# Layer 1 of a four-layer graph kernel attends first and projects the aggregate; VectorE takes four late copies

## The chip, the cores and the metric

The kernel runs on one core of one Trainium2 chip. The metric is the device time of one execution in microseconds. The core has five engines that run their own instruction queues in order and meet at semaphores: TensorE (PE, matrix products into eight PSUM banks), VectorE (DVE), ScalarE (ACT), GpSimd (POOL, which reads and writes SBUF alone here) and SyncE (SP, which issues the transfers of the loop).

## The reference, cut to what matters

`x` is 128 graphs x 128 nodes x 256 features, `adj` one 128x128 matrix for all graphs. Four layers follow, each on `h = relu(layernorm(x))` and each added to `x`:

```python
x = x + L0(h)   # deg * (h Wi^T + b) + adj @ (h Wj^T)
x = x + L1(h)   # single-head attention over nodes, below
x = x + L2(h)   # single-head attention, 128 wide, [alpha @ hh, hh]
x = x + L3(h)   # eight-head attention with q, k, v and output projections

def L1(x, adj, W, a_src, a_dst):
    Wh = einsum('bnd,de->bne', x, W)
    e_src = einsum('bnd,d->bn', Wh, a_src)
    e_dst = einsum('bnd,d->bn', Wh, a_dst)
    logits = leaky_relu(e_src[:, :, None] + e_dst[:, None, :], 0.2)
    logits = where(adj == 0, -inf, logits)
    return einsum('bnm,bmd->bnd', softmax(logits), Wh)
```

## The kernel before

Graphs are handled in pairs (`G = 2`), so there are 64 of them. Nodes lie on the 128 partitions and a pair is 512 columns of f32. In steady state every engine runs `step(t)`, a fixed list of operations, each on the pair `t - LAG[operation]`: one step starts layer 0 of a new pair and ends layer 3 of one eight steps older. `fill()` and `drain()` hold the same operations written out for the first and last pairs. All these lists and the lags, as well as `BANKS`, which says in which PSUM bank a task writes and which operations free it, were laid out ahead of time. `passed` waits for an operation to have reached a pair, `bank_free` for the last user of a bank, `read_before` for the readers of a buffer (most buffers hold two pairs, those of the scores of layer 3 one).

Products that must be exact use a split: a matrix is kept as an upper part rounded to `fp32r` and a lower remainder, and `split_matmul` (L1565 to L1567) adds three products, upper times upper, upper times lower, lower times upper. The products of attention and all transposes are in f32 (each f32 product shows as two instructions, a transpose as one).

Layer 1 of a pair goes as follows. DVE takes statistics of x1, POOL makes `y1 = (x1 - mean) * rstd` (`normalise`, L440). PE transposes y1 (`transpose_y`, L1575, four transposes of 128x128). ACT takes relu and the upper part (L1230), DVE the lower part (`relu_transposed_low`, L821). `project1` multiplies by W, extended by two columns W a_src and W a_dst (258 columns), into one bank per graph; ACT copies both to `wh` (`copy_projection1`, L1258). Column 257 is the destination's logit of every node: POOL gathers it (`gather_dst`, L463), SP writes it to memory and reads it back spread over all partitions (for the first four and last five pairs `spread_dst` does this by a transpose, L1654). ACT adds the source's logit and applies leaky relu (`sum_logits`, L1284), DVE masks it and takes the row's extreme in one `tensor_tensor_reduce` (`mask_logits`, L831), ACT takes exponentials and their sum (L1293), PE transposes them (`transpose_exp`, L1662), ACT copies them (L1301), and `attend` (L1670) multiplies them with `wh`: two f32 products of 256 columns. DVE scales by the inverse sum and adds x1 (`sum_x2`, L847).

Layer 2 has the same stages with 128 columns; its attention product is L1670 with `hh`, its sum `sum_x3` L857, its projection `project2` L1646. Layer 3 projects q, k and v; `add_bias` on DVE (L866) copies q and k from their banks, with the bias; `scores` (L1707) fills four banks, DVE masks them (`mask_scores`, L874), ACT takes exponentials (L1315), POOL normalises (L469), PE transposes four banks (L1715), ACT copies them (`copy_p3_transposed`, L1323), `attend3` (L1727) and `project4` (weights `wo`) follow, and DVE adds (L897).

On PE the step's list is, in order: `project0(1)`, `project4`, the projections to k and q, `project0(0)`, transposes for layers 2 and 3 of older pairs, `attend` of layer 2, `project2`, the transposes of y1, `scores`, `attend3`, the transposes of layer 1's exponentials, `project_v`, `project1(1)`, `attend` of layer 1, `project1(0)`, the transposes of y3, `aggregate`, two more banks of transposed probabilities.

## Time and profile before

| | us |
|---|---|
| time, median of 3 runs | 1220.35 (1220.34 to 1221.02) |
| time of the profiled execution | 1220.8 |
| span from its first to its last instruction | 1218.8 |
| PE busy | 1200.7 (99%) |
| ACT busy | 1082.4 (89%) |
| POOL busy | 1068.4 (88%) |
| DVE busy | 1053.9 (86%) |
| TensorE clock granted, mean share of full speed | 0.999 |

The busy time of an engine counts instructions that do work, not waits. Matmuls overlap in the pipeline of the array, so the time that one costs is read from the start of one to the start of the next, not from its duration.

### The profile page before, as it was taken

What the parts mean: (1) busy time and instruction counts of PE and PEld (TensorE: products, weight loads), DVE (VectorE), ACT (ScalarE), POOL (GpSimd) and SP (SyncE); (2) the same over time, 40 slices, a digit from 0 to 9 for tenths busy, and PEclk for the clock granted to TensorE, in tenths of its full rate; (3) what the DMA queues carried; (4) which work ended last, traced back from release to release, by engine and by line L of the source; (5) the groups of instructions that cost most, each with busy time, mean ns of one, the idle gap of its engine ahead of it and who ended that gap; (6) DMA issues with size and microseconds to landing.
All of it is one profiled execution on the core that took longest, in us unless ns stands there. A gap on an engine that the chain in (4) does not pass through costs nothing.

```text
span 1218.8 us, 43750 instructions
## 1 busy us (share of the span) xinstructions
PE 1200.7 (99%) x12017; PEld 1108.6 (91%) x12017; DVE 1053.9 (86%) x5142; ACT 1082.4 (89%) x3976; POOL 1068.4 (88%) x1848
## 2 busy tenths in 40 slices
PE   8999999999999999999999999999999999999997
PEld 7789999999999999999999999999999999999986
DVE  6898898898898898888988988988988888988874
ACT  3679898898898898898998998998998998998997
POOL 5998899899899898999899899899899899898774
PEclk9999999999999999999999999999999999999999
DMA  7333333343442433534333332432433343330001
GB/s 187 63 46 51 77 68 55 79 67 57 77 67 57 77 67 55 79 64 60 77 63 60 77 65 58 75 68 59 71 69 60 69 67 66 67 51 26 20 20 36
DMA packets 97678, 78.57 MB, mean 64 GB/s; under 512 B 31648, under 2 KB 89248, under 8 KB 97440
## 3 DMA queue, kind: packets, MB, share of 16 engines
q1 hardware_dynamic: 94960, 74.07, 32.9%
q8 instruction: 102, 1.67, 0.8%
q14 instruction: 136, 1.11, 0.6%
q10 hardware_dynamic: 2480, 1.71, 0.5%
HBM read 58.79 MB, written 16.95 MB: 62 GB/s over the span
## 4 chain that ended last, share of the span: by engine, by line
PE 90%; issue 1%; DVE 1%; POOL 0%; ACT 0%; POOLq 0%; DVEq 0%; ACTq 0%
PE bank L1565 16%; PE bank L1567 16%; PE bank L1566 16%; PE bank L1715 9%; PE bank L1670 6%; PE bank L1575 6%; PE bank L1707 6%; PE bank L1727 5%; PE bank L1646 4%; PE bank L1662 3%; PE bank L1626 2%; POOL probs L469 0%; ACT exps L1315 0%; DVE masked L874 0%; PE bank L1654 0%
## 5 line engine op out<-in xcount | busy, mean ns | idle before, releaser
L1315 ACT ACTIVATE exps<-masked,nmax 128x128 f32<-128x128 f32 x1024 | 396.8, 393 | 0.9 <-DVE nmax L874 0.4
L469 POOL TENSOR_TENSOR probs<-exps,rsum 128x512 f32<-128x512 f32 x256 | 266.3, 1042 | 16.2 <-DVE rsum L882 15.7
L440 POOL TENSOR_SCALAR y<-x,nm,rstd 128x256 f32<-128x256 f32 x384 | 212.0, 560 | 31.5 <-issue 31.0
L874 DVE CUSTOM_DVE_ANT_0 masked<-bank,mask 128x128 f32<-128x128 f32 x1024 | 227.4, 284 | 0.8 <-PE bank L1707 0.5
L1315 ACT ACTIVATION_READ_ACCUMULATOR exps<-masked,nmax 128x1 f32 x1024 | 197.3, 193 | 0.0
L760 DVE BATCH_NORM_STATS2 stats<-x 128x6 f32<-128x256 f32 x512 | 190.4, 414 | 4.6 <-DMA x<-in_x 4.4
L1565 PE MATMUL bank<-w_hi,ht_hi 128*128 128x512 f32 (+1 forms) x508 | 189.4, 373 | 0.4 <-DVE ht_lo L821 0.3
L417 POOL TENSOR_TENSOR rstd<-veps,power 128x2 f32<-128x2 f32 x256 | 182.7, 714 | 5.3
L1567 PE MATMUL bank<-w_hi,ht_lo 128*128 128x512 f32 (+1 forms) x508 | 172.6, 340 | 0.0
L1566 PE MATMUL bank<-w_lo,ht_hi 128*128 128x512 f32 (+1 forms) x508 | 172.5, 340 | 0.0
L1323 ACT ACTIVATE probs3t<-bank 128x512 f32<-128x512 f32 x256 | 145.0, 595 | 0.7 <-PE bank L1715 0.7
L1715 PE MATMUL bank<-ident,probs 128*128 128x128 f32 x1024 | 134.3, 273 | 1.2 <-DVE nmax L874 0.8
L1252 ACT ACTIVATE mj_hi<-bank,rstd 128x256 fp32r<-128x256 f32 x128 | 59.8, 468 | 81.5 <-PE bank L1567 78.0
L1715 PEld LDWEIGHTS bank<-ident,probs 128*128 128x128 f32 x1024 | 117.3, 141 | 10.8 <-issue 2.2
L1575 PE MATMUL bank<-ident,y 128*128 128x128 f32 x768 | 115.6, 273 | 4.2 <-POOL y L440 4.1
L1293 ACT ACTIVATE ez<-z,nmax 128x128 f32<-128x128 f32 x256 | 100.2, 394 | 8.0 <-DVE nmax L831 4.4
L1567 PEld LDWEIGHTS bank<-w_hi,ht_lo 128*128 128x128 f32 x508 | 96.1, 189 | 11.7
L781 DVE SCALAR_TENSOR_TENSOR mj_lo<-bank,rstd,mj_hi 128x256 fp32r<-128x256 f32 x128 | 61.2, 479 | 52.6 <-ACT mj_hi L1252 52.5
L1565 PEld LDWEIGHTS bank<-w_hi,ht_hi 128*128 128x128 f32 x508 | 96.6, 190 | 9.3 <-DVE ht_lo L821 1.1
L1566 PEld LDWEIGHTS bank<-w_lo,ht_hi 128*128 128x128 f32 x508 | 96.8, 191 | 7.6
L1575 PEld LDWEIGHTS bank<-ident,y 128*128 128x128 f32 x768 | 89.7, 141 | 6.2 <-POOL y L440 5.7
L857 DVE SCALAR_TENSOR_TENSOR x<-bank,rsum,x 128x128 f32<-128x128 f32 x128 | 39.0, 347 | 60.7 <-PE bank L1670 59.1
(136 smaller groups left out, 3970.4 us busy)
## 6 DMA issues: line engine op xcount, KB each, us to landing
x<-in_x SPq DMA_DIRECT2D x64, 256.0 KB, 5.9
xt_sb<-in_xt SPq DMA_DIRECT2D x64, 256.0 KB, 5.7
out<-x SPq DMA_DIRECT2D x64, 256.0 KB, 5.7
db<-rows SPq DMA_DIRECT2D x110, 128.0 KB, 4.1
mean_b<-rows SPq DMA_DIRECT2D x62, 128.0 KB, 3.4
rows<-dst SPq DMA_DIRECT2D x110, 1.0 KB, 3.6
rows<-mv SPq DMA_DIRECT2D x62, 1.0 KB, 5.8
probs<-in_w0t ACTq DMA_DIRECT2D x1, 256.0 KB, 3.5
```

The lines of the kernel that those rows point to most:

```text
L417: pool.tensor_tensor(rstd[i][:, b], veps[i][:, b], power[:], ALU.pow).then_inc(S[f"rstd{i}"], 1)
L440: last = pool.tensor_scalar(y[i][:, b, g], src[:, bx, g], nm[i][:, s, g:g + 1], rstd[i][:, s, g:g + 1], ALU.add, ALU.mult)
L469: pool.tensor_tensor(probs3[:, p % BUFFERS["probs3"], j], exps3[:, p % BUFFERS["exps3"], j], rsum3[:, s, j].unsqueeze(2).to_broadcast([P, ...
L760: last = dve.bn_stats(stats[i][:, b, g], src[:, bx, g])
L874: last = dve.tensor_tensor_reduce(masked3[:, b, j, i], bank_of(f"sc{j}")[:, i * P:(i + 1) * P], mask[:], scale=-1.0, scalar=-MASKED, op0=A ...
L1315: last = act.activation(exps3[:, b, j, i], masked3[:, p % BUFFERS["masked3"], j, i], ACT.Exp, bias=nmax3[:, s, j, i:i + 1], scale=-1.0, ac ...
L1323: act.activation(probs3t[:, b, j].rearrange("p b n -> p (b n)"), bank_of(f"pt{j}")[:], ACT.Copy).then_inc(S[f"p3t_{j}"], 1)
L1565: pe.matmul(out_ap, lhs[0], rhs[0], start=start, stop=False)
L1566: pe.matmul(out_ap, lhs[0], rhs[1], start=False, stop=False)
L1567: return pe.matmul(out_ap, lhs[1], rhs[0], start=False, stop=stop)
L1575: last = pe.transpose(bank_of(f"h{i}t")[:, (c * G + g) * P:(c * G + g + 1) * P], y[i][:, b, g, c * P:(c + 1) * P], ident[:])
L1715: last = pe.transpose(bank_of(f"pt{j}")[:, i * P:(i + 1) * P], probs3[:, p % BUFFERS["probs3"], j, i], ident[:])
```

## The change

What is computed stays the same. Layer 1 uses that `softmax(..) @ (h W)` is `(softmax(..) @ h) W`, and that `h = relu(x1 - mean) * rstd`, since rstd is positive.

- POOL makes `y1 = max(x1 - mean, 0)` (`centre1`), without rstd.
- The two logits of a node are products of its row with the vectors W a_src and W a_dst. PE spreads these over all partitions of bank 6 once at the start (`a1_rows`), and the bank holds nothing else from then on. DVE makes four `tensor_tensor_reduce` of 256 columns per pair (`logit_products1`), POOL multiplies the four columns of results by rstd (`scale_logits1`). SP writes the destination's logits from there; the gather on POOL is gone.
- The transposes of y1, relu and split of the transposed y1 and the copies to `wh` are gone.
- ACT's copy of layer 1's transposed exponentials multiplies by rstd of the source node, which is its partition there, so one copy becomes two. `aggregate1` multiplies y1 with it, four f32 products of 128 columns whose result is already transposed. ACT and DVE split it (`high_g1`, `low_g1`), and `project1` makes both graphs' 12 products of 256 columns into one bank, from which `sum_x2` reads as before.
- The bias of k is added by ACT (`add_key_bias`) in place of DVE.
- Of the last two pairs, DVE copies banks 2 and 3 of the transposed probabilities, ACT banks 0 and 1.
- x1 and y1 have three buffers in place of two. The tasks share banks 0 to 5 in place of 0 to 6, and the lists of every queue, `fill()`, `step()` and `drain()`, are in a new order, with new lags (the last projection of a pair comes one step later). On PE: `aggregate1`, transposes of y2, of layer 2's exponentials, two banks of probabilities, `attend` of layer 2, `project2`, `scores`, `attend3`, `project1`, `project_v`, a bank of probabilities, `aggregate`, transposes of y3, a bank of probabilities, transposes of layer 1's exponentials, `project0(1)`, `project4`, `project0(0)`, q, k.

```diff
-    "kt": (0, "kt_mm", ('kt',)),
-    "qt": (3, "qt_mm", ('qt',)),
-    "m0": (2, "m0", ('mj_lo0', 't0_0')),
-    "at2": (4, "e2t", ('at2',)),
-    "h2t": (5, "h2t", ('ht2',)),
-    "pt0": (6, "pt0", ('p3t_0',)),
...
+    "d1": (4, "d1", ('z1',)),
+    "g1": (3, "g1_mm", ('g1_lo',)),
+    "h2t": (2, "h2t", ('ht2',)),
+    "at2": (1, "e2t", ('at2',)),
+    "pt3": (4, "pt3", ('p3t_3',)),
+    "pt0": (5, "pt0", ('p3t_0',)),
+    "x3b": (1, "x3_mm", ('x3',)),
+    "hh": (0, "hh_mm", ('hh',)),
...
+    "sc3": (1, "scores", ('nmax3_3',)),
+    "ot": (0, "ot_mm", ('ot_lo',)),
+    "x2b": (3, "x2_mm", ('x2',)),
+    "v": (5, "v_mm", ('v',)),
+    "pt2": (2, "pt2", ('p3t_2',)),
+    "x1b": (0, "s0", ('x1',)),
+    "h3t": (1, "h3t", ('h3t_lo',)),
+    "pt1": (3, "pt1", ('p3t_1',)),
+    "at1": (5, "e1t", ('at1',)),
+    "m1": (2, "m1", ('mj_lo1', 't0_1')),
+    "x4b": (0, "x4_mm", ('x4',)),
+    "d2": (3, "d2", ('z2',)),
+    "m0": (5, "m0", ('mj_lo0', 't0_0')),
+    "qt": (1, "qt_mm", ('qt',)),
+    "kt": (0, "kt_mm", ('kt',)),
...
+        a1_rows = bank[6]
...
+                passed(sp, "sd1", p)
...
+                sp.dma_start(rows[1][b], logits1[:, p % SMALL, 1]).then_inc(row_out[1][b], 16)
...
+            def centre1(p):
+                b, s, bx = p % BUFFERS["y1"], p % SMALL, p % BUFFERS["x1"]
+                passed(pool, "nm1", p)
+                read_before(pool, "y1", p, "dots1", "g1_mm")
+                for g in range(G):
+                    last = pool.tensor_scalar(y[1][:, b, g], x1[:, bx, g], nm[1][:, s, g:g + 1], 0.0, ALU.add, ALU.max)
+                last.then_inc(S["y1"], 1)
+
+            def scale_logits1(p):
+                s = p % SMALL
+                passed(pool, "dots1", p)
+                passed(pool, "rstd1", p)
+                passed(pool, "z1", p, SMALL)
+                pool.tensor_tensor(logits1[:, s], dots1[:, s], rstd[1][:, s].unsqueeze(1).to_broadcast([P, 2, G]), ALU.mult).then_inc(S["sd1"], 1)
...
+            def logit_products1(p):
+                b, s = p % BUFFERS["y1"], p % SMALL
+                passed(dve, "y1", p)
+                dve.wait_ge(S["products"], 1)
+                passed(dve, "dots1", p, 1)
+                passed(dve, "sd1", p, SMALL)
+                for g in range(G):
+                    for k in range(2):
+                        last = dve.tensor_tensor_reduce(products1[:, k, g], a1_rows[:, k * D:(k + 1) * D], y[1][:, b, g], scale=1.0, scalar=0.0,
+                                                        op0=ALU.mult, op1=ALU.add, accum_out=dots1[:, s, k, g:g + 1])
+                last.then_inc(S["dots1"], 1)
+
+            def low_g1(p):
+                b = p % BUFFERS["ht1"]
+                passed(dve, "g1_hi", p)
+                read_before(dve, "ht1", p, "x2_mm")
+                dve.tensor_tensor(ht1_r[1][:, b].rearrange("p c g n -> p (c g n)"), bank_of("g1")[:],
+                                  ht1_r[0][:, b].rearrange("p c g n -> p (c g n)").bitcast(F32), ALU.subtract).then_inc(S["g1_lo"], 1)
...
+            def copy_late_p3_transposed(j, p):
+                b = p % BUFFERS["probs3t"]
+                passed(dve, f"pt{j}", p)
+                read_before(dve, "probs3t", p, "ot_mm")
+                dve.tensor_copy(probs3t[:, b, j].rearrange("p b n -> p (b n)"), bank_of(f"pt{j}")[:]).then_inc(S[f"p3t_{j}"], 1)
...
+                copy_late_p3_transposed(2, NP - 2)
+                sum_x4(NP - 3)
+                copy_late_p3_transposed(3, NP - 2)
                 inverse_sum3(2, NP - 1)
-                inverse_sum3(1, NP - 1)
-                sum_x4(NP - 3)
+                inverse_sum3(3, NP - 1)
+                copy_late_p3_transposed(2, NP - 1)
...
+                if due(t, "dots1"):
+                    logit_products1(t - LAG["dots1"])
+                if due(t, "x3"):
+                    sum_x3(t - LAG["x3"])
...
-            def copy_projection1(g, p):
-                b = p % BUFFERS["wh"]
-                passed(act, f"wh{g}_mm", p)
-                read_before(act, "wh", p, "x2_mm", "z1")
-                act.activation(wh[:, b, g], bank_of(f"wh{g}")[:, 0:D + 2], ACT.Copy).then_inc(S[f"wh{g}"], 1)
+            def high_g1(p):
+                b = p % BUFFERS["ht1"]
+                passed(act, "g1_mm", p)
+                read_before(act, "ht1", p, "x2_mm")
+                act.activation(ht1_r[0][:, b].rearrange("p c g n -> p (c g n)"), bank_of("g1")[:], ACT.Copy).then_inc(S["g1_hi"], 1)
+
+            def copy_exp_transposed1(p):
+                b, s = p % BUFFERS["at1"], p % SMALL
+                passed(act, "e1t", p)
+                passed(act, "rstd1", p)
+                read_before(act, "at1", p, "g1_mm")
+                for g in range(G):
+                    last = act.activation(at[1][:, b, g], bank_of("at1")[:, g * P:(g + 1) * P], ACT.Copy, scale=rstd[1][:, s, g:g + 1])
+                last.then_inc(S["at1"], 1)
+
+            def add_key_bias(p):
+                b = p % BUFFERS["kt"]
+                passed(act, "kt_mm", p)
+                read_before(act, "kt", p, "scores")
+                for c in range(DC):
+                    last = act.activation(kt[:, b, c], bank_of("kt")[:, c * G * P:(c + 1) * G * P], ACT.Identity, bias=bk_sb[:, c:c + 1])
+                last.then_inc(S["kt"], 1)
...
+                for k in range(2):
+                    for e in range(DC):
+                        pe.matmul(a1_rows[:, k * D:(k + 1) * D], a1_sb[:, e, k:k + 1].to_broadcast([P, P]), w1t_sb[:, e, :], start=(e == 0), stop=(e == DC - 1))
...
+            def aggregate1(p):
+                b, bt = p % BUFFERS["y1"], p % BUFFERS["at1"]
+                passed(pe, "at1", p)
+                bank_free(pe, "g1", p)
+                for c in range(DC):
+                    for g in range(G):
+                        last = pe.matmul(bank_of("g1")[:, (c * G + g) * P:(c * G + g + 1) * P], y[1][:, b, g, c * P:(c + 1) * P], at[1][:, bt, g],
+                                         start=True, stop=True)
+                last.then_inc(S["g1_mm"], 1)
+
+            def project1(p):
                 b = p % BUFFERS["ht1"]
-                passed(pe, "h1t_lo", p)
+                passed(pe, "g1_lo", p)
                 pe.wait_ge(S["w1_split"], 1)
-                bank_free(pe, f"wh{g}", p)
-                for c in range(DC):
-                    last = split_matmul(bank_of(f"wh{g}")[:, 0:D + 2], [h_[:, b, c, g] for h_ in ht1_r], [w_[:, c, :] for w_ in w1_r],
-                                        c == 0, c == DC - 1)
-                last.then_inc(S[f"wh{g}_mm"], 1)
+                bank_free(pe, "x2b", p)
+                for g in range(G):
+                    for c in range(DC):
+                        last = split_matmul(bank_of("x2b")[:, g * D:(g + 1) * D], [h_[:, b, c, g] for h_ in ht1_r], [w_[:, c, :] for w_ in w1_r],
+                                            c == 0, c == DC - 1)
+                last.then_inc(S["x2_mm"], 1)
```

## Rows read from the trace of the kernel before

**Rows 1.** The page, first part: busy time, share, instructions.
```profile
PE 1200.7 (99%) x12017; PEld 1108.6 (91%) x12017; DVE 1053.9 (86%) x5142; ACT 1082.4 (89%) x3976; POOL 1068.4 (88%) x1848
```
**Rows 2.** Stretches: window, length, busy time by engine, clock, DMA, GB/s.
```profile
150.00:1100.00 950.00, 950.00 (x9628) 881.25 (x9627) 841.26 (x4138) 869.21 (x3206) 860.54 (x1496) 1.00 0.37 66
...
1150.00:1185.00 35.00, 34.27 (x378) 32.34 (x376) 26.33 (x140) 33.70 (x133) 24.80 (x37) 1.00 0.07 24
```
**Rows 3.** Waits, 150 to 1100 us: who waited, releaser, total, times, longest.
```profile
ACT mj_hi L1252 <- PE bank L1567: 67.1, 51, 1.4
DVE x L857 <- PE bank L1670: 51.3, 52, 1.2
DVE mj_lo L781 <- ACT mj_hi L1252: 48.3, 50, 1.0
```
**Rows 4.** PE in order of time, one period: start, duration, engine, line, count.
```profile
603.30 0.28 PE L1565 MATMUL bank<-wo_hi,ot_hi 128*128 128x256 f32 x1
...
610.45 0.61 PE L1670 MATMUL bank<-hh,at 128*128 128x128 f32 x4
610.90 1.06 PE L1646 MATMUL bank<-w_sb,ht 128*128 128x130 f32 x8
611.80 0.60 PE L1575 MATMUL bank<-ident,y 128*128 128x128 f32 x4
612.36 1.17 PE L1707 MATMUL bank<-kt,qt 32*128 32x128 f32 x32
...
621.68 0.28 PE L1565 MATMUL bank<-wo_hi,ot_hi 128*128 128x256 f32 x1
```
**Rows 5.** PE in order of time, near the end.
```profile
1172.06 1.06 PE L1646 MATMUL bank<-w_sb,ht 128*128 128x130 f32 x8
1173.05 1.17 PE L1707 MATMUL bank<-kt,qt 32*128 32x128 f32 x32
```
**Rows 6.** The chain of waits, in order of time: start, length, what.
```profile
1148.59 0.86 PE bank L1670 x4
```
**Rows 7.** PE in order of time, at the start.
```profile
16.69 1.11 PE L1560 MATMUL bank<-exps,bv_sb 128*128 128x256 f32 x4
17.45 0.58 PE L1626 MATMUL bank<-mj_hi,aggr_r 128*128 128x512 f32 x1
```
**Rows 8.** DVE's groups by shape: count, busy us, mean ns, idle before.
```profile
L821 DVE SCALAR_TENSOR_TENSOR ht_lo<-bank,ht_hi 128x512 fp32r<-128x512 f32 x128 | 86.5, 676 | 2.7 <-ACT ht_hi L1230 2.4
L874 DVE DVE_READ_ACCUMULATOR2_ANT nmax<- 128x1 f32 x1024 | 85.9, 84 | 0.0
...
L866 DVE TENSOR_SCALAR kt<-bank,bk_sb 128x256 f32<-128x256 f32 x128 | 55.5, 476 | 0.7 <-PE bank L1567 0.7
```
**Rows 9.** DVE in order of time, masking of scores.
```profile
614.30 0.29 DVE L874 CUSTOM_DVE_ANT_0 masked<-bank,mask 128x128 f32<-128x128 f32 x1
...
614.51 0.29 DVE L874 CUSTOM_DVE_ANT_0 masked<-bank,mask 128x128 f32<-128x128 f32 x1
```
**Rows 10.** ACT's groups by shape.
```profile
L1323 ACT ACTIVATE probs3t<-bank 128x512 f32<-128x512 f32 x256 | 145.0, 595 | 0.7 <-PE bank L1715 0.7
...
L1252 ACT ACTIVATE mj_hi<-bank,rstd 128x256 fp32r<-128x256 f32 x128 | 59.8, 468 | 81.5 <-PE bank L1567 78.0 <-PE bank L1616 3.4
...
L1301 ACT ACTIVATE at<-bank 128x256 f32<-128x256 f32 x128 | 47.6, 372 | 0.3 <-PE bank L1662 0.3
L1258 ACT ACTIVATE wh<-bank 128x258 f32<-128x258 f32 x128 | 42.0, 379 | 3.1 <-PE bank L1567 3.1
...
L1284 ACT ACTIVATE bank<-bank,hh 128x128 f32<-128x128 f32 x18 | 5.4, 338 | 2.1 <-DVE ht_lo L814 2.1
```
**Rows 11.** DVE in order of time, at layer 2's sum.
```profile
611.10 0.61 DVE L857 SCALAR_TENSOR_TENSOR x<-bank,rsum,x 128x128 f32<-128x128 f32 x2 [0.98 <-PE bank L1670]
```
**Rows 12.** PE's waits from 1100 us on.
```profile
PE bank L1707 <- DVE x L857: 0.8, 1, 0.8
```
**Rows 13.** ACT's loads of its function table.
```profile
L1209 ACT ACT_TABLE_LOAD x1 | 1.3, 1283 | 4.0 <-issue 4.0
```

More of the change, by code:

```diff
@@ L368, in _ @@
             fill()
-            for t in range(17, NP + 12):
+            for t in range(15, NP + 10):
                 step(t)
@@ L701, in _ @@
             fill()
-            for t in range(9, NP + 4):
+            for t in range(6, NP + 2):
                 step(t)
@@ L1194, in _ @@
             fill()
-            for t in range(11, NP + 6):
+            for t in range(11, NP + 7):
                 step(t)
@@ L1283, in sum_logits @@
                         logits = db[i][:, p % 2].rearrange("p (n g) -> p g n", g=G)[:, g]
-                    last = act.activation(bank_of(f"zz{i}")[:, (G + g) * P:(G + g + 1) * P], logits, ACT.Prelu, bias=src[:, bs, g, col:col + 1], alpha=SLOPE)
+                    last = act.activation(bank_of(f"zz{i}")[:, (G + g) * P:(G + g + 1) * P], logits, ACT.Prelu, bias=own[:, g:g + 1], alpha=SLOPE)
                 last.then_inc(S[f"z{i}"], 1)
@@ L1653, in spread_dst @@
                 for g in range(G):
-                    last = pe.transpose(bank_of(f"d{i}")[:, g * P:(g + 1) * P], src[:, b, g, col:col + 1].to_broadcast([P, P]), ident[:])
+                    last = pe.transpose(bank_of(f"d{i}")[:, g * P:(g + 1) * P], own[:, g:g + 1].to_broadcast([P, P]), ident[:])
                 last.then_inc(S[f"d{i}"], 1)
```

1247 lines of the change are left out of this document (580 added, 667 removed), and 26 rows, old and new, of the table LAG.

## The prediction

> **What bounds the kernel now.** I read the engines' shares first. The tensor engine (PE) is busy 99% of the span, no other engine over 89% [rows 1]. Then the stretches, since a share over the span hides its parts: from 150 to 1100 us PE is busy for all of 950 us, at a granted clock of 1.00 (2.4 GHz), while VectorE (DVE) has 841.3, ScalarE (ACT) 869.2 and GpSimd (POOL) 860.5 us [rows 2]. The waits of the same stretch name who waits for whom: ACT and DVE wait for PE, and PE for nobody [rows 3]. So in the steady part a nanosecond taken from PE is a nanosecond of the kernel, until another engine is late.
>
> The order in time gives the price of one pair of graphs. The output projection of one pair starts at 603.30, of the next at 621.68: 18.38 us [rows 4]. Scaled to that period, DVE works 841.3 / 950 x 18.38 = 16.28 us, ACT 16.82 and POOL 16.65. These are the reserves: 2.1, 1.6 and 1.7 us per pair. They are not free to use in any place, since each engine runs a fixed order: ACT waits 67.1 us in 51 places (1.3 us a pair) for one product of layer 0, DVE 51.3 us in 52 (1.0 us a pair) for layer 2's attention product and 48.3 us (0.9) for ACT's copy [rows 3].
>
> The pieces do not overlap as their durations suggest (a matmul that lasts 0.28 us is followed 0.12 us later by the next), so PE is priced from start to start.
>
> **PE: what leaves.** The four transposes of y1 go. Before the scores, a layer norm's four transposes start at 611.80 and the scores at 612.36: 0.56 us. But what follows matters: in the steady order projection 2, transposes, scores take 612.36 - 610.90 = 1.46 us [rows 4]; near the end, where there is no transpose between them, projection 2 to scores takes 1173.05 - 1172.06 = 0.99 us [rows 5]. So the transposes are worth 0.47 us per pair, not 0.56. Twelve products of 258 columns become twelve of 256, under 1% of each: 0.01 us. Together 0.48.
>
> **PE: what comes.** The attention product of layer 1 was two f32 products of 256 columns (4 instructions, 0.86 us in the chain [rows 6]). It becomes four of 128 columns. Layer 2 has two of just that width, 610.90 - 610.45 = 0.45 us [rows 4], so four are 0.90: 0.04 more. The net gain is 0.44 us per pair, a new period of 17.94 us, and 64 x 0.44 = 28.2 us over the kernel. Bounds: 0.35 (the 0.09 between the two prices of the transposes could be lost elsewhere as well) to 0.56 (their full slot), thus 22 to 36 us. PE is idle 18.1 us in all (1218.8 - 1200.7), at the two ends, so nearly all pairs count in full.
>
> At the start, four products of 256 columns (they spread the folded attention vectors over bank 6) replace eight of two columns. Two such products took 17.45 - 16.69 = 0.76 us [rows 7], so four 1.5 us; against this stands what the small ones took. Between 0 and 1.5 I take +0.7, as PE has a first full chain to wait for anyway.
>
> **DVE.** Per pair leave: the lower half of the transposed h1 (0.68) and the biased copy of k (2 x 55.5/128 = 0.87) [rows 8]. The lower half of the new aggregate comes, same shape, 0.68. New are four multiply-and-reduce instructions of 256 columns with one operand in PSUM. No such row exists, but the masking of the scores is the same instruction at 128 columns: one starts at 614.30, the next at 614.51, its accumulator read in between [rows 9]. That is 0.21 us. The next 128 elements cost 0.10 us by the step from 256 to 512 columns (0.476 to 0.676 for 256 elements), 0.19 by the step from 128 to 256 (0.29 to 0.476): 0.31 to 0.40 each; I take 0.35, four are 1.4. From above: a 256-column instruction out of PSUM with a mean of 0.476 and a separate accumulator read of 0.084 [rows 8], 0.56 each and 2.24 for four; from below four at the 128-column price, 0.85. I take 1.4, since it starts from the row of the same instruction. DVE's work becomes 16.28 - 0.87 + 1.4 = 16.8 us, at worst 17.65.
>
> A rule stands against this price. The Trainium skill (VectorE: DVE Perf Modes, "The TRN2 errata - SBUF-src ops pay a fixed extra latency per instruction") gives a VectorE instruction out of PSUM 120 cycles and one per element at 0.96 GHz. By it one new instruction is an estimated 0.39 us, four 1.57, and DVE would stand at 17.0. At 128 columns it gives 0.26 where this trace shows 0.21, so I stay with the row; either leaves DVE under 17.94.
>
> **ACT.** Leave: two copies of wh (2 x 42.0/128 = 0.66) and one 256-column copy of the transposed exponentials (0.37). The upper half of the aggregate replaces that of h1, equal shape, nothing. Come: two 128-column copies with a scale per partition (0.30 each by the 128-column pass, 0.60; from below half of 0.372 each, 0.37) and k with its bias, two of 256 columns (0.74 by the plain copy, 0.94 by the scaled one; I take 0.80, near the plain one) [rows 10]. Net +0.37, bounds +0.1 to +0.6: ACT at 17.2 us, at worst 17.4.
>
> **POOL.** The normalisation of layer 1 keeps its two instructions, without the factor; a small gather goes and a small multiplication comes. I count nothing; bounded by 0.2 us either way, since both are a few elements. It stands at 16.7 us. On SyncE the row of logits is now written straight from what POOL made, one hop fewer.
>
> **Cover that is gone.** At 17.94 the reserves are DVE 1.1, ACT 0.7, POOL 1.3 us, against forced waits of 1.9, 1.3 and little. They cannot all stay; where an engine runs late, PE waits. I allow 0.04 us per pair, 2.5 us, from nothing to 0.3. The banks for all this fall from seven to six, another reason for some waits.
>
> **The end.** From 1150 to 1185 us ACT is busy 33.7 of 35 [rows 2]. Four copies of 0.60 us [rows 10] move from it to DVE (26.3 of 35 busy), of which only two stand ahead of the last exponentials; k's biased copies come in. Net I take -1 us, between -2.4 and +0.8.
>
> **The sum**, against the profiled execution (span 1218.8, its time 1220.8): 1220.8 - 28.2 + 0.7 + 2.5 - 1 = 1194.8. The median of before is 0.45 lower than that execution: 1194.3, say 1194.
>
> **Rivals.**
> 1. *PE stays the bound, as summed.* 1188 to 1201. For it: 950 of 950 us and all three others below the new period. Chance 0.70.
> 2. *The reserves do not suffice.* ACT at its upper 17.4, with part of its 1.3 us wait for layer 0's product still forced, or a bank not yet emptied, sets 18.1 to 18.25 us per pair. The gain is then 0.13 to 0.28 us over 64 pairs: 8 to 18 us, so 1202 to 1217. Against it: the order on all queues is new and may lay the waits elsewhere. Chance 0.17.
> 3. *No change*, within 0.2% (2.4 us, what a measurement of this kernel can tell): the reserves of rival 2 fail wholly, at 18.38 again. Chance 0.04.
> 4. *Slower: DVE late at layer 2's sum.* The scores write the bank that layer 2's attention product used, and must wait for DVE to have read it. Today DVE stands waiting 0.98 us for that product and then takes 0.61 us; at the end of the kernel PE did wait 0.8 us for it once [rows 11, 12]. In the new order the four reductions stand right in front of this sum in DVE's queue, and the transposes that covered it are gone. If DVE's work and its 0.98 us wait both stay, the period is their sum: 16.8 + 0.98 = 17.8, still under 17.94. From a price of 0.50 us per reduction (four at 2.0) it is 18.38, no gain; at the upper bound, 17.65 + 0.98 = 18.63, or +0.25 x 64 = 16 us: 1236. Against: the same instruction's row is far below. Chance 0.07.
> 5. *Slower: ACT reloads its function table.* k's bias is added by an Identity activation, which no row of before shows; the one load at the start took 1.28 us [rows 13]. Two loads per pair would put ACT at 17.2 + 2.6 = 19.8 us: 64 x 1.4 = 90 us more, near 1311. For it nothing but the absence of a row. Chance 0.02. The Trainium skill (ScalarE: Activation LUTs, "Table sets: the hidden batching unit") has identity in every set, so that by it no load comes; no row of before shows it.
>
> **How the numbers follow.** Predicted 1194. The range takes rival 1 whole and most of rival 2: 1186 to 1215; outside lie rivals 3 to 5 and a rest of the others, together 0.17. Faster by over 0.2%: 0.70 + 0.17 = 0.87. Same 0.04. Slower 0.07 + 0.02 = 0.09.
>
> **What would show it.** Right: distance between two output projections 17.9 to 18.0 us in the steady part; no PE wait of weight from 150 to 1050 us; projection 2 to scores 0.99 us; layer 1's attention 0.90 us; the new reduction 0.35 us from start to start; one table load; DVE near 16.8 and ACT near 17.2 us per pair. Wrong: PE waits in every pair, above all at the scores for DVE's sum of layer 2 (rival 4) or at a bank that ACT empties (rival 2); reductions of 0.5 us and more; ACT or DVE over 98% of a stretch with PE under it.

## The result, and the profile after

After: 1235.54 us, median of 4 runs (1234.37 to 1237.49); before, on the same chip, 1220.68 (1220.34 to 1221.17). The ratio is 1.0123, 95% interval [1.0105, 1.0141]: 1.2% slower, where I had forecast 2.2% faster. The profiled execution's span is 1232.6 us. Two executions of this document were disturbed, one of e9 (2981.98 us) and one of the kernel before beside e18 (1690.15 us), and the ratios leave them out.

The page's shares and the stretch 150 to 1100 us of the kernel after (columns of the second: stretch, its length, busy time of PE, PEld, DVE, ACT, POOL with instruction counts, granted clock, DMA share, GB/s) stand against [rows 1] and [rows 2]:

```profile
PE 1189.9 (97%) x12017; PEld 1098.7 (89%) x12017; DVE 1095.0 (89%) x5528; ACT 1098.1 (89%) x4036; POOL 1136.8 (92%) x1857
```
```profile
0.00:30.00 30.00, 19.90 (x108) 16.70 (x108) 18.49 (x63) 9.98 (x18) 16.95 (x31) 0.92 0.74 187
30.00:60.00 30.00, 23.86 (x127) 19.75 (x126) 25.65 (x105) 16.68 (x49) 27.62 (x45) 0.91 0.40 76
...
150.00:1100.00 950.00, 940.07 (x9615) 871.46 (x9616) 874.13 (x4440) 880.93 (x3254) 913.25 (x1501) 1.00 0.39 66
```

PE no longer works without a gap (940 of 950 us), and POOL has risen from 860.5 to 913.25. The mean distance between two pairs is now 18.41 us (1012.5 / 55, from the table below), so POOL works 913.25 / 950 x 18.41 = 17.70 us per pair, DVE 16.94 and ACT 17.07. I had forecast 16.7, 16.8 and 17.2. The groups by shape in the same stretch name what grew on POOL, and show the new work of DVE and ACT (busy us, mean ns | idle before):

```profile
L461 POOL TENSOR_SCALAR y<-x,nm 128x256 f32<-128x256 f32 x102 | 116.7, 1153 | 5.0
L453 POOL TENSOR_SCALAR y<-x,nm,rstd 128x256 f32<-128x256 f32 x207 | 113.9, 557 | 8.9 <-issue 8.9
...
L833 DVE CUSTOM_DVE_ANT_0 products<-bank,y 128x256 f32<-128x256 f32 x204 | 74.1, 420 | 0.1
...
L1300 ACT ACTIVATE kt<-bank,bk_sb 128x256 f32<-128x256 f32 x102 | 41.6, 458 | 0.0
L1292 ACT ACTIVATE at<-bank,rstd 128x128 f32<-128x128 f32 x104 | 32.5, 373 | 0.0
```

The first two lines are the answer. Layers 2 and 3 still normalise (add a column, multiply by a column) at 0.557 us an instruction. Layer 1's centring (add a column, then the maximum with 0) has the same shape, source and destination and takes 1.153. Two per pair are 1.19 us more than what they replaced.

That alone would still fit: 16.65 + 1.19 = 17.84, under the forecast period of 17.94. What busy time hides is seen in POOL's own waits from 150 to 1100 us, of the kernel before, then of after, then of e1 below (each time the largest entry that names another engine: total, times, longest):

```profile
POOL dst L463 <- ACT wh L1258: 20.3, 46, 0.7
```
```profile
POOL dst L491 <- ACT hh L1313: 5.3, 6, 1.5
```
```profile
POOL dst L491 <- ACT hh L1313: 50.6, 51, 1.7
```

With the smaller entries POOL waits for others 22.7 us of the 950 in the kernel before, though it is busy only 860.5: 0.44 us per pair, not the 1.7 us that the busy share suggests. The rest of its idle time lies between its own instructions. In the kernel after, it waits 5.3 us in all, and its centrings of two pairs start 18.27 us apart nearly throughout, 0.57 us more than its work. That is POOL's own period, and it is longer than the 17.94 that I forecast.

Where the time lies: I date each pair by PE's product of the messages of layer 0. The span is then the time to the ninth of them (pair 8), 55 periods, and the rest.

| span, us | to pair 8 | 55 periods | after pair 63 | sum |
|---|---|---|---|---|
| before | 122.3 | 1012.1 | 84.4 | 1218.8 |
| after | 118.7 | 1012.5 | 101.4 | 1232.6 |
| centring as multiplication (e1, below) | 110.6 | 1001.5 | 101.4 | 1213.5 |

The new order holds one pair more in flight: it is filled sooner and drained about a period (17 us) later. But the periods gained nothing. Undisturbed ones lie at 18.07 to 18.30 us: PE runs at 18.1 while it makes up for a late pair, and at POOL's 18.27 once it has. Now and then one is 1 to 2 us longer. Those have a sign of their own, ACT waiting for a row of layer 2 that comes back from memory (waits of the stretch, total, times, longest; then one such wait):

```profile
ACT bank L1326 <- DMA db<-rows: 24.9, 14, 3.3
...
PEld bank L1600 <- POOL y L453: 7.4, 22, 0.4
```
```profile
769.22 0.68 ACT L1326 ACTIVATE bank<-db,hh 128x128 f32<-128x128 f32 x2 [3.30 <-DMA db<-rows]
```

In the kernel before the same wait was 3.3 us in all. What POOL itself loses in such a period it cannot make up, as it has nothing left to wait for.

In the fill POOL's centring stands ahead of work for which DVE, and by it PE, wait (start, us, engine, line):

```profile
22.94 2.70 POOL L461 TENSOR_SCALAR y<-x,nm 128x256 f32<-128x256 f32 x2
25.60 0.19 POOL L438 TENSOR_TENSOR degr<-rstd,deg 128x2 f32<-128x2 f32 x1
...
25.93 0.48 DVE L798 SCALAR_TENSOR_TENSOR t<-bank,degr,r 128x256 f32<-128x256 f32 x1 [2.06 <-POOL degr L438]
...
28.23 0.79 PE L1651 MATMUL bank<-mj_hi,aggr_r 128*128 128x512 f32 x1 [5.43 <-DVE mj_lo L789]
```

PE's idle time before 150 us goes from 8.7 to 23.0 us. How much of it is the centring's, e1 tells: 13.8 us remain with the cheap one, pair 8 comes 8.1 us sooner, and the wait of 5.43 us only falls to 4.2. The granted clock in the first two stretches is 0.92 and 0.91 (before: 0.94 and 1.00), a mean over parts at 1.2 and parts at 2.4 GHz. PE had been idle since 22.8 us when it fell to 1.2 GHz; these two parts of the kernel after stand against one in the kernel before, 24.6 to 27.9 us:

```profile
25.20:31.90 6.70, 3.48 (x9) 2.37 (x10) 5.97 (x26) 1.80 (x4) 6.44 (x12) 0.50 0.29 46
45.70:49.00 3.30, 3.30 (x15) 3.01 (x14) 3.23 (x15) 1.41 (x6) 3.11 (x4) 0.50 0.29 75
```

### The profile page after: what moved, and what is told of

It is laid out like the page before. It is cut to its first block and busy times, and to the rows that moved or that the text cites. A ratio compares the mean times of both kernels' runs of the same rounds, so it can differ in the third digit from the quotient of the medians.

```text
span 1232.6 us, 44146 instructions
## 1 busy us (share of the span) xinstructions
PE 1189.9 (97%) x12017; PEld 1098.7 (89%) x12017; DVE 1095.0 (89%) x5528; ACT 1098.1 (89%) x4036; POOL 1136.8 (92%) x1857
## 5 line engine op out<-in xcount | busy, mean ns | idle before, releaser
L1357 ACT ACTIVATION_READ_ACCUMULATOR exps<-masked,nmax 128x1 f32 x1024 | 200.0, 195 | 0.0
L1590 PE MATMUL bank<-w_hi,ht_hi 128*128 128x512 f32 (+1 forms) x508 | 184.0, 362 | 0.0
L461 POOL TENSOR_SCALAR y<-x,nm 128x256 f32<-128x256 f32 x128 | 146.9, 1156 | 6.0
L453 POOL TENSOR_SCALAR y<-x,nm,rstd 128x256 f32<-128x256 f32 x256 | 140.9, 557 | 10.8 <-issue 10.4
L1750 PE MATMUL bank<-ident,probs 128*128 128x128 f32 x1024 | 143.7, 273 | 0.6 <-POOL probs L497 0.6
L1590 PEld LDWEIGHTS bank<-w_hi,ht_hi 128*128 128x128 f32 x508 | 95.9, 189 | 18.0 <-issue 11.7
L833 DVE CUSTOM_DVE_ANT_0 products<-bank,y 128x256 f32<-128x256 f32 x256 | 93.0, 420 | 6.4 <-POOL y L461 6.3
L476 POOL TENSOR_TENSOR r<-x,deg_b 128x512 f32<-128x512 f32 x64 | 82.2, 1286 | 5.6 <-DVE t L798 5.5
L858 DVE CUSTOM_DVE_ANT_0 z<-bank,mask 128x128 f32<-128x128 f32 x256 | 62.9, 283 | 27.4 <-ACT bank L1326 26.8
```

Of the source, the lines that this page charges most:

```text
L453: last = pool.tensor_scalar(y[i][:, b, g], src[:, bx, g], nm[i][:, s, g:g + 1], rstd[i][:, s, g:g + 1], ALU.add, ALU.mult)
L461: last = pool.tensor_scalar(y[1][:, b, g], x1[:, bx, g], nm[1][:, s, g:g + 1], 0.0, ALU.add, ALU.max)
L1357: last = act.activation(exps3[:, b, j, i], masked3[:, p % BUFFERS["masked3"], j, i], ACT.Exp, bias=nmax3[:, s, j, i:i + 1], scale=-1.0, ac ...
L1590: pe.matmul(out_ap, lhs[0], rhs[0], start=start, stop=False)
L1750: last = pe.transpose(bank_of(f"pt{j}")[:, i * P:(i + 1) * P], probs3[:, p % BUFFERS["probs3"], j, i], ident[:])
```

## Experiments

All ratios are to the kernel before on the same chip, with 95% intervals; "base" is the kernel after unless another is named.

### What makes the centring slow

**e1.** The same instruction, add and multiply (the ReLU of layer 1 is left out).

```
-  tensor_scalar(y1, x1, nm1[g], 0.0,      ALU.add, ALU.max)
+  tensor_scalar(y1, x1, nm1[g], power[g], ALU.add, ALU.mult)
```

> The changed kernel, but layer 1's centring on GpSimd multiplies by a constant per partition instead of taking the maximum with 0 (the relu of layer 1 is left out, so its values differ). In the trace of the changed kernel the two centring instructions last 1.156 us each, the normalisations, which multiply, 0.557. Theory P (GpSimd is the bound): the two instructions fall to 0.56 us each, GpSimd's period of 18.28 us falls under that of TensorE, and the time goes to 1192 to 1203 us. Rival R (the new order: late rows of layer 2's logits, and banks): GpSimd is not what sets the period, the time stays at 1228 to 1237. Rival D (VectorE late at layer 2's sum): also 1228 to 1237.

Measured: 1216.57 us, ratio 0.9961 [0.9947, 0.9975].

```profile
150.00:1100.00 950.00, 945.42 (x9698) 883.04 (x9697) 881.70 (x4486) 884.72 (x3287) 858.62 (x1513) 1.00 0.40 66
```
```profile
L461 POOL TENSOR_SCALAR y<-x,nm,power 128x256 f32<-128x256 f32 x105 | 57.2, 555 | 5.2
```

One operation is worth 19 us, and with it the change is 0.4% faster than before. In the traces 8.1 of the 19.1 us lie ahead of pair 8 and 11.0 in the 55 periods. POOL now waits for others 59.4 us of the 950, so its own period is (950 - 59.4) / 950 x 18.21 = 17.07 us, and 17.07 + 1.19 = 18.26 is what the kernel after showed. It is not 1194, though, nor even inside my range, which ended at 1215: PE's own period comes out at 18.13 us and not 17.94, so a second step of mine was off.

**e2.** The 0 of the maximum read from a column (`zero1[g]`) in place of an immediate.

> The changed kernel, but the 0 of the maximum comes from a column of zeros in memory instead of a constant of the instruction. Theory M (the maximum is the slow operation on GpSimd): 1.15 us each as before, time 1230 to 1238. Theory I (a constant beside a pointer is slow): 0.56 us each, time as in the run with the multiplication, 1192 to 1203.

1239.66 us, 1.0155 [1.0134, 1.0175], a little over theory M's 1238; 1.234 us an instruction. The kind of operand is not the cause. And the run shows who sets the pace: 2 x (1.234 - 1.153) = 0.16 us more on POOL, and its centrings start 18.44 us apart where they were 18.27, with PE's undisturbed periods at the same 18.44.

**e11, e14.** Two forms each, one per graph (e11: the ReLU is left out of the second graph; e14: out of both, and the second graph's value is another).

```
e11  g0: (x1, mean, nm,  ALU.max, ALU.add)    g1: (x1, nm, None, ALU.add)
e14  g0: (x1, nm, 1.0,   ALU.add, ALU.mult)   g1: (x1, power, nm, ALU.mult, ALU.add)
```

> A measurement of what the centring instruction costs on GpSimd by its operations. Of each pair the first graph is centred as maximum with the mean, then minus the mean (the same value as the ReLU of the difference), the second graph as one addition of the negative mean with no second operation (its ReLU is left out). In the kernel after both are addition, then maximum, at 1.15 us each; addition, then multiplication took 0.56 us. Theory M (the maximum is slow wherever it stands): the first graph's takes 1.1 to 1.3 us, the second's 0.5 to 0.6. Rival O (only the maximum as second operation is slow): both take 0.5 to 0.6 us, and the time falls to about 1217. Rival T (a fast form exists only for a pair of add and multiply, or for two pointers): both take 1.1 us or more.

> A measurement of the centring instruction on GpSimd by its form (the ReLU is left out of both graphs, and the second graph's value is another: -0.5 x minus mean). First graph: addition of the mean's column, then multiplication by an immediate 1. Second graph: multiplication by a column, then addition of a column. So far: add column, multiply column 0.56 us; add column alone 0.94; add, maximum 1.16; maximum, add with two columns 1.24. Theory A (add and multiply is what is cheap, in either order and with either kind of operand): both take 0.50 to 0.62 us. Rival C (cheap is only add, then multiply, with two columns): the first takes 1.1 to 1.2 us, the second 1.2 to 1.3. Rival O (the order decides, the kind of operand does not): the first 0.56, the second 1.2.

POOL's answers by shape from 150 to 1100 us, of e11 and then of e14:

```profile
L460 POOL TENSOR_SCALAR y<-x,mv,nm 128x256 f32<-128x256 f32 x52 | 64.3, 1237 | 5.2
L461 POOL TENSOR_SCALAR y<-x,nm 128x256 f32<-128x256 f32 x52 | 48.7, 936 | 0.0
```
```profile
L461 POOL TENSOR_SCALAR y<-x,power,nm 128x256 f32<-128x256 f32 x52 | 29.1, 559 | 0.0
L460 POOL TENSOR_SCALAR y<-x,nm 128x256 f32<-128x256 f32 x52 | 24.7, 476 | 5.1
```

All three theories of e11 missed: even an addition alone takes 0.94 us, more than addition and multiplication together. e14 fits the theory that add with multiply is cheap in either order (the immediate form, at 0.476, is a little cheaper still). So it is not that the maximum is dear; that pair is cheap. Why it is, no run shows. (One run each: 1222.31 and 1217.04 us.)

**e4.** Base: the kernel before, with add and maximum on POOL in layer 1 (the factor is left out, so the logits are not the reference's).

> The kernel before, but GpSimd's two instructions for layer 1 subtract the mean and take the maximum with 0 instead of multiplying by the inverse deviation (layer 1 is then computed from rows that are not scaled, so values differ). They should take 1.16 us each in place of 0.56, GpSimd's work goes from 16.65 to 17.85 us a pair. Theory P: still under TensorE's 18.38, so the steady part keeps its period; 1220 to 1230 us, the rise coming from the first pairs, where GpSimd is behind. A theory by which GpSimd's order, not its sum, decides: TensorE waits in every pair, 1235 us and more.

1271.33 us, 1.0417 [1.0402, 1.0433], against my 1220 to 1230. The old order takes the same 1.2 us far worse, although POOL is busy only 883 of 950 us (columns as above; then two waits):

```profile
150.00:1100.00 950.00, 912.78 (x9189) 844.78 (x9188) 802.97 (x3953) 847.30 (x3072) 882.97 (x1439) 1.00 0.37 65
```
```profile
DVE x L860 <- POOL r L459: 85.8, 49, 2.1
...
PE bank L1710 <- DVE t L793: 36.8, 49, 1.5
```

POOL hands over late in each pair, DVE waits, PE waits for DVE. But POOL itself waits for other engines only 2.3 us of the 950, down from 22.7: it is full, at 93% busy. Its 0.44 us of true reserve are used up and the rest of the 1.19 us lengthens the period, 18.38 + 1.19 - 0.44 = 19.13, which is the distance measured in nearly every pair. The engine's own sequence sets the period here as in the kernel after.

### The centring elsewhere

**e3, e10, e13.** On DVE, right before its products: as add and maximum (e3), the same with a tensor of zeros as second input (e10, `scalar_tensor_tensor`), and as add and multiply (e13; the ReLU is left out).

> The changed kernel, but VectorE does the centring and relu of layer 1, one operation ahead of the mask that stands before the four reductions. Theory P: GpSimd drops by 2.3 us a pair to 15.4, VectorE rises from 16.9 to 17.4 or 17.6 (two instructions of 0.25 to 0.35 us), TensorE sets the period again at 17.95 to 18.1: 1192 to 1206 us. Rival R: 1228 to 1237. Rival D: VectorE is later still at layer 2's sum, waits of TensorE at the scores in every pair, 1236 to 1260.

> VectorE does the centring as in the earlier run (1262.7 us), but with a second input tensor of zeros for the maximum. In that run the two instructions took 0.88 us each, three times what the 256 elements need, while GpSimd worked. Theory S (the one-tensor form reads through a second port that GpSimd also uses, and waits for it): with two inputs 0.40 to 0.48 us each, VectorE's work falls by 0.8 us a pair, and TensorE's wait for layer 2's sum at the scores (0.9 us a pair) goes down by as much: 1212 to 1235 us. Rival (256 elements from memory cost VectorE 0.88 in any form): 1255 to 1266.

> The centring stands on VectorE, as addition of the negative mean, then multiplication by a constant column (its ReLU is left out). The same two instructions as addition, then maximum, took 0.88 us each there, and on GpSimd the pair add and multiply took 0.56 where add and maximum took 1.16. Theory A (what is slow is every pair of operations but add and multiply, on both engines): VectorE's instruction takes 0.3 to 0.45 us, VectorE is busy some 17.8 us per pair, and the time is 1217 to 1232, well under the 1262.7 of the maximum on VectorE. Rival V (VectorE takes 0.85 us or more for a subtraction of this shape from memory in any form, and only GpSimd has a cheap pair): the instruction takes 0.8 to 0.95 us and the time is 1258 to 1266.

e3 1262.68 us, 1.0342 [1.0317, 1.0366]; e10 1280.79, 1.0491 [1.0454, 1.0528]; e13 1266.86, 1.0374 [1.0344, 1.0405]. e3 came nearest its rival D (1236 to 1260), e13 its rival V (1258 to 1266); in e10 both theories missed. On DVE the operation makes no difference (0.88 us busy on average with the maximum, 0.94 with the multiplication), so theory A fell there. The spread of e13's instruction (min/median/max in ns) and one pair of them beside POOL's work show something else:

```profile
L814 DVE TENSOR_SCALAR y<-x,nm,power x99: 402/1125/1430, 165.3 to 1099.9; 128x256 f32<-128x256 f32 x99
```
```profile
603.61 1.30 POOL L445 TENSOR_TENSOR xt_sb<-xt_sb,mean_b 128x512 f32<-128x512 f32 x1 [0.77 <-DMA mean_b<-rows]
603.78 2.33 DVE L814 TENSOR_SCALAR y<-x,nm,power 128x256 f32<-128x256 f32 x2
604.87 1.08 POOL L489 TENSOR_TENSOR probs<-exps,rsum 128x512 f32<-128x512 f32 x1
```

DVE's two instructions span 603.78 to 606.11, and POOL's two end at 604.91 and 605.95: each of DVE's ends 0.15 us behind one of POOL's. From 150 to 1100 us this holds for every one that took over 0.6 us, 68 of 68 in e3 and 72 of 72 in e13; the one of each run that met no instruction of POOL over 0.4 us took 344 and 402 ns. The reductions right behind them, with one operand in PSUM, stay at 409 to 422 ns in both. That is the picture of an exclusive resource. The Trainium skill (SBUF — State Buffer, "SBUF: two separate sides") describes one: a VectorE operation in a two-port mode, or with two inputs in SBUF, and a GpSimd operation that reads SBUF block each other for the whole instruction. The traces agree, by the ends and by the jump from 402 to 1125 ns; so does e10, with two such inputs (median 1243 ns). e10's theory S took the two-input form for a way round the shared port; its miss speaks against that form and not against the port. And the chain of my rival 4 appears in e3, as I had described it:

```profile
PE bank L1743 <- DVE x L875: 43.4, 49, 1.8
```

**e5.** One graph's centring on POOL (maximum), the other's on ACT (Relu with a bias); complete.

> The changed kernel with the whole of its arithmetic, but ScalarE does the centring and relu of one of the two graphs (a Relu with the negative mean as bias), GpSimd the other. GpSimd falls by one instruction of 1.156 us to 16.5 us a pair, ScalarE rises from 17.07 by 0.3 to 0.37 to 17.4. Theory P: as in the run with the multiplication, TensorE's own period of 18.10 us rules, 1212 to 1220 us, under the 1220.9 of before. Rival (ScalarE has no such reserve in its fixed order): 1222 to 1236.

1232.47 us, 1.0091 [1.0064, 1.0119]: theory P missed, the rival holds. The undisturbed period fell to 18.13, as POOL has 55.9 us of waits for others again. But against e1 pair 8 came 11.0 us later, at 121.6, and the 55 periods lost 6.7 us more to lengthened ones (1008.2 us); what in ACT's new place does that was not tried.

### POOL's sum, eased without touching the centring's operations

**e8, e12.** POOL scales the degrees of pairs 1 and 2 before it centres pair 0 (e8 on e1, e12 on the kernel after).

> The kernel with the centring as add and multiply (its ReLU is left out) and one change of order: in the fill GpSimd scales the degrees of pairs 1 and 2 before it centres pair 0, right behind their inverse deviations, where the kernel after has them behind it. In the kernel after, TensorE stands 5.43 us at 28.23 us and 1.48, 1.28 and 2.15 us at 35.42, 37.65 and 45.42 us, and the first of these follows from VectorE's t of pair 1, which waited for a degree that stood behind 2.70 us of centring. Theory F (the fill loses time to GpSimd's order): the first of these waits falls from 5.7 to about 3.5 us or less, the aggregate of pair 8 comes at 107 to 109 us in place of 110.6, and the time is 2 to 3 us under that of the kernel with the order as it was: 1213.5 to 1215. Rival G (the fill is bound by VectorE or by the loads, and GpSimd's order only names the last of several late things): the aggregate of pair 8 stays at 110 to 111 us and the time stays at 1216.6 within 1.5 us.

> The kernel after, complete, with GpSimd scaling the degrees of pairs 1 and 2 before it centres pair 0, and nothing else changed. By theory F the fill's first long wait of TensorE (5.43 us at 28.23 us) loses 2.5 us or more, and the time falls from 1235.5 to 1232 to 1233.5 (GpSimd is the bound in the steady part, so all of what the fill gives back is kept only if the centrings of the later pairs come earlier too). By rival G the time stays within 1.5 us of 1235.5. In neither case does it reach the kernel before.

1215.16 us, 0.9957 [0.9942, 0.9972], and 1232.12, 1.0100 [1.0083, 1.0117]. Neither is clear of its base's interval, though e12's median is 3 us lower. In the traces pair 8 comes at 110.9 us in e8 (110.6 in e1) and at 118.6 in e12 (118.7 in after), and PE's two waits for mj_lo only fell from 5.7 to 5.3 us and from 6.9 to 6.5. The fill gave nothing back: theory F fell.

**e16, e17.** On e12: layer 1's centring subtracts the mean itself, so that POOL's `nm1` (0.23 us) goes (e16); all three layers do (e17). Both complete.

```
-  tensor_scalar(y1, x1, nm1[g],  0.0, ALU.add,      ALU.max)
+  tensor_scalar(y1, x1, mean[g], 0.0, ALU.subtract, ALU.max)
```

> Complete. The kernel after, with the degrees of pairs 1 and 2 scaled earlier in the fill (that alone gave 1232.1), and layer 1's centring subtracts the mean where it stands, so that GpSimd's instruction that makes the negative mean (0.23 us per pair) is gone. GpSimd then has 17.5 us of work per pair and not 17.7. If GpSimd's sum is what holds the period, the ordinary period falls to TensorE's 18.13, the periods lengthened by late rows are made up sooner, the fill is shorter by 0.23 us for each of its first pairs: 1226 to 1229. If GpSimd were no longer the bound in this kernel, 1231 to 1233. A subtraction in place of an addition may also have another price beside the maximum: at 1.25 us each or more the time would not fall.

> Complete. As the kernel without layer 1's negative mean, and the normalisations of layers 2 and 3 subtract the mean as well (subtract, then multiply with two columns), so that all three instructions of 0.23 us leave GpSimd. Theory A extended (subtract and multiply is as cheap as add and multiply, 0.56 us): GpSimd has 17.0 us per pair, half a microsecond over the 16.5 of the kernel with the multiplication, which took 1215 to 1217: the time is 1217 to 1222, about that of the kernel before. Rival (only add with multiply is cheap): the normalisations take 1.0 to 1.25 us each, GpSimd 18.9 to 19.6 us per pair, and the time is 1275 or more.

e16: 1223.23 us, 1.0014 [0.9994, 1.0034]: level with the kernel before, the best complete version in the new order, and under its forecast of 1226 to 1229. POOL's sum fell 0.23 us per pair and 9 us of time came back by the medians (10 by the two ratios); POOL's own period would be 18.27 - 0.23 = 18.04, and undisturbed periods are PE's 18.13. The trace doesn't show the 9 us: it is of an execution of 1227.4 us, high in a spread from 1220.6 to 1229.5, and its 55 periods take 1008.1 us, with ten lengthened ones, where e12's take 1008.4. e17: 1328.51, 1.0868 [1.0846, 1.0889]: its rival holds. POOL's line of e16, then of e17:

```profile
L461 POOL TENSOR_SCALAR y<-x,mv 128x256 f32<-128x256 f32 x104 | 118.0, 1142 | 0.3 <-DVE mv L773 0.3
```
```profile
L453 POOL TENSOR_SCALAR y<-x,mv,rstd 128x256 f32<-128x256 f32 x190 | 231.3, 1223 | 8.2 <-issue 8.2
```

Subtract and multiply costs 1.22 us where add and multiply costs 0.56, and the period is 20.00 us in nearly every pair.

### The row of layer 2

**e9.** On e1: the row is spread from a constant input, with no wait for the write (layer 2's logits are not the reference's). **e18.** On e16, complete: the row is written straight from the projection, in 256 pieces of 4 bytes, without POOL's gather.

> The kernel with the centring as add and multiply, and the row of layer 2's neighbour terms is spread from an input in memory (a bias of 256 numbers) in place of the row that was written for it, so that the spreading waits for no write; the write itself stays. The output is not the reference's in layer 2's attention. Theory R (the round trip of the row through memory is what makes the irregular periods: ScalarE waits 15.4 us in 11 places for it in the stretch 150 to 1100): that wait falls under 3 us, the mean period falls from 18.21 to 18.10 us, which is TensorE's own, and the time is 4 to 6 us under 1216.6: 1210 to 1213. Rival S (the row is late since the queue of transfers is busy with the loads and stores issued just ahead of it): the wait stays at 8 us or more and the time at 1214 to 1218.

> Complete. The kernel without layer 1's negative mean (1223.2 us, where the kernel before took 1222.9), and layer 2's neighbour terms are written to memory straight from the projection's tile by the transfer, in 256 pieces of 4 bytes, so that GpSimd's copy that gathers them (0.19 us per pair) is gone too. GpSimd then has 17.3 us of work per pair, and the row starts on its trip up to 1.6 us earlier, as it waits no more behind GpSimd's other work. If GpSimd's sum and the late row (23.7 us of waits of ScalarE in 13 places) are what lengthens some periods, those waits fall under 15 us and the time falls by 2 to 5 us, to 1218 to 1221, just under the kernel before. Rival (the many small pieces make the write itself slower, and the row is later than it was): the waits rise above 30 us and the time is 1225 or more.

e9: 1220.71 us, 0.9995 [0.9979, 1.0010]. The wait for the row is down to 3.7 us and another transfer is late in its place; both theories missed, and it is slower than e1:

```profile
DVE stats L771 <- DMA x<-in_x: 39.0, 28, 2.9
```

e18: 1321.48 us, 1.0841 [1.0821, 1.0860]; its rival holds, far more strongly than I put it. SyncE's queue waits for the write, and all loads behind it are late:

```profile
SPq L293 <- DMA rows<-hh: 241.7, 47, 6.7
```
```profile
DVE stats L757 <- DMA x<-in_x: 134.1, 47, 3.8
```

In the kernel after that wait of the queue was 102.6 us in 51 places, 2.0 us each; with the small pieces it is 5.1.

### The late copies, and one price on PE

**e6.** On e1: ACT makes all four late copies as before. **e7.** The kernel before with DVE making them.

> The first run (multiplication in the centring, relu left out, 1216.6 us) with the late copies undone: ScalarE copies all four banks of the last two pairs. By the forecast's term the copies are worth 1 us (0.8 less to 2.4 more): end from the last aggregation 1 to 2.4 us longer than its 101.3 us. Rival: nothing, as the last pair waits for the normalisation on GpSimd.

> The kernel before with this part of the change alone: VectorE copies banks 2 and 3 of the transposed probabilities of the last two pairs. Forecast's term: 0.5 to 2.4 us less, 1218.5 to 1220.4, from an end of 84.4 us after the last aggregation. Rival: the same time within 0.3 us.

e6: 1221.33 us, 0.9993 [0.9974, 1.0011]; e7: 1221.00, 0.9994 [0.9984, 1.0003]. In the traces the part after pair 63 goes from 101.4 to 102.1 us without them in the new order, and from 84.4 to 84.2 with them in the old. So 0.7 and 0.2 us; e6's ratio against e1's, taken on another chip, allows more.

**e15.** The kernel before, complete, with each attention product of 256 columns issued as two of 128.

> The kernel before, complete, with each of layer 1's two f32 attention products of 256 columns issued as two of 128 columns into the same places; nothing else changed. TensorE bounds this kernel in every period. My prediction priced this step at +0.04 us per pair (0.90 against 0.86). In the kernel after the eight instructions of four such products take 0.89 us from start to start, where the four of before took 0.67. Theory N (the narrow products cost what the start to start intervals say): the group takes 0.87 to 0.92 us, the period goes from 18.38 to 18.58 to 18.62 us, and the time rises by 13 to 15 us, to 1233.5 to 1236. Rival K (my term of the prediction: the longer interval is only a load of weights that shows at another place): the period rises by 0.04 and the time by 2 to 4 us, to 1222.5 to 1224.5.

1221.93 us, 1.0012 [1.0002, 1.0021]: 1.3 us, and the period is 18.40 to 18.44. Theory N fell and my term stands, though the time is just under rival K's range. PE's order in one period shows why the intervals misled me:

```profile
617.10 1.05 PE L1672 MATMUL bank<-wh,at 128*128 128x128 f32 x8
617.91 0.37 PE L1565 MATMUL bank<-w_hi,ht_hi 128*128 128x258 f32 x1
```

The group took 0.81 us from start to start where it took 0.67, and the six products behind it 0.82 where they took 0.92: part of one group's time shows in the next.

## Why the prediction was wrong, step by step

- **POOL, the step that failed.** "The normalisation of layer 1 keeps its two instructions, without the factor ... I count nothing; bounded by 0.2 us either way". I bounded the small gather and left the two large instructions unpriced, since a factor was only taken away. They cost 2 x (1.153 - 0.557) = 1.19 us per pair. Shown by e1: 19 us back by the operation alone, of the 41 between 1194 and 1235.5.
- **POOL's reserve, read wrongly.** "These are the reserves: 2.1, 1.6 and 1.7 us per pair" took all that is not busy for reserve. By its waits for others POOL had 0.44 us in the kernel before, and in the new order its own period is 18.27 us with the maximum and 17.07 without. Against 17.94 its reserve was thus 17.94 - 18.27 = -0.33, and would have been 0.87, not 1.3. Shown by e2 (18.44) and e4 (19.13), which follow from it to 0.01 us. With the right price and the wrong reserve I would still have forecast a gain.
- **PE's gain, the second step that failed.** Forecast 0.44 us per pair, measured with POOL relieved 18.38 - 18.13 = 0.25. In e1's order (below) projection 2 to scores takes 613.04 - 611.96 = 1.08 us, not the 0.99 of [rows 5]; against 1.46 in [rows 4] the transposes are worth 0.38, not 0.47. The narrow products are as priced (e15). The last 0.1 is spread over groups of less than 0.1 each and is not settled. Over the kernel this is 10 us, and with the ends it put even e1 outside my range.

```profile
611.51 0.61 PE L1705 MATMUL bank<-hh,at 128*128 128x128 f32 x4
611.96 1.06 PE L1682 MATMUL bank<-w_sb,ht 128*128 128x130 f32 x8
613.04 0.72 PE L1742 MATMUL bank<-kt,qt 32*128 32x128 f32 x15
```

- **Cover.** I allowed 2.5 us. Once POOL is relieved, 1001.5 - 55 x 18.13 = 4.4 us are lost to lengthened periods, so near, and in the bounds. The three longest of e1 each hold a wait of ACT of 2.3 to 3.0 us for a row from memory. That they come from transfers and not from ACT or DVE I had not seen.
- **Start and end.** Forecast -0.3 us together. By the table of parts, fill and drain together went from 206.7 to 212.0 us even in e1, where 9 periods' gain should have taken 4 off: 9 us worse. The drain is 17.0 us longer and the fill only 11.7 shorter. In e1 PE is idle 5 us more before 150 us than in the kernel before, and it is at 1.2 GHz for some 10 us in place of 3.4; how the 9 us divide among this and the longer chain was not tried. I had read only one late stretch of ACT.
- **DVE and ACT were right.** The new reduction starts 0.345 us apart (forecast 0.35), DVE stands at 16.94 (16.8), ACT at 17.07 (17.2). By the rule of the Trainium skill that the prediction cites the reduction was an estimated 0.39: the trace decides for the row. No second table load appears, so rival 5 is out. The late copies bring 0.2 to 0.7 us by the traces.
- **The rivals.** None of mine had POOL as its place. Rival 4's chain is real (e3), but needed 1.8 us more on DVE. Rival 2's form, an engine a little short, came true with another engine and no gain left; its range does not follow from its own gain of 8 to 18 us, which gives 1202 to 1212 and not 1217. That e1's 1216.6 lies in 1202 to 1217 is luck: there PE's own period is the bound.

The sum, corrected: 1194.8, plus 10 us for PE's period (55 x 0.19), 2 for cover, 9 for the ends is 1216, e1's time; plus 19 for POOL is 1235.

## What to carry to other kernels

Price every instruction whose operations change, even where one only goes away: same shape, engine and operands bound nothing. Read an engine's reserve from the time that it waits for others, not from what its busy share leaves: the gaps between its own instructions are no reserve. In the old order POOL's 1.19 us met 0.44 us of such waits and the period rose by 0.75; in e1 they met 17.07 against PE's 18.13, and the undisturbed period rose by 0.14, the rest of the 19 us being fill (8 us) and lengthened periods (3 us).

## What the hardware showed unexpectedly

GpSimd's tensor_scalar on 128 x 256 f32, mean ns by its operations (from after, e1, e2, e11, e14, e16, e17): add column, multiply by an immediate 476; add, multiply by columns 555; multiply, add by columns 559; add alone 936; subtract, maximum with an immediate 1142; add, maximum with an immediate 1153; subtract, multiply by columns 1223; add, maximum by columns 1234; maximum, add by columns 1237. The Trainium skill (GPSIMD Engine Reference, "Engine selection") calls one-input operations roughly line-rate; these rows differ by 2.6 times at one input, so here the operations decide. The periods confirm the durations: e2's 0.16 us more on GpSimd lengthened the distance of its centrings by 0.17, and from e1 to after its own period grew by 1.20 for 1.19.

On DVE the instruction's 402 ns become 1125 in the middle case beside a busy GpSimd, and each long one ends 0.15 us behind an instruction of GpSimd.
